# Summing the scan's states in turned form in both loop halves of a decoder kernel, with the work behind it one loop step later

## The reference, cut to what matters

```python
u = silu(x_proj); dt = softplus(u @ W_dt + b_dt); Bm, Cm = split(u @ W_x + b_x)
def step(h, inp):                       # over the 128 tokens
    h = h * exp(dt_t[..., None] * A) + (dt_t * u_t)[..., None] * B_t[:, None, :]
    y_t = einsum('bds,bs->bd', h, C_t) + D_param * u_t
    return (h, y_t)
y = y * silu(z)
return y @ W_out + b_out
```

## Time and profile before

| | |
|---|---|
| median of 3 executions | 391.0 us (390.95 to 392.38) |
| the profiled execution, whole | 391.27 us |
| its span in the trace | 389.3 us |
| TensorE busy with matmuls | 326.6 us (84%) |
| VectorE busy | 309.9 us (80%) |
| GpSimd busy | 217.4 us |
| ScalarE busy | 213.5 us |
| the scan loop | first scan starts at 157.2 us, last at 280.0 us |

### The profile page before, as it was taken

One profiled execution on the slowest core, in us unless ns is written; L12 is line 12 of the kernel. 1 busy time (PEld: TensorE's weight loads), 2 busy tenths in 40 slices (PEclk: granted clock), 3 DMA queues, 4 the chain that ended last, 5 costly groups with the idle time before them and its releaser, 6 DMA issues. The chain is left out here.

```text
span 389.3 us, 5280 instructions
## 1 busy us (share of the span) xinstructions
PE 326.6 (84%) x1666; PEld 227.7 (58%) x1666; DVE 309.9 (80%) x630; ACT 213.5 (55%) x467; POOL 217.4 (56%) x223
## 2 busy tenths in 40 slices
PE   5636929779768889889998998988799989999992
PEld 2432419778546465533343586555598857989872
DVE  0799999998666977999999989999958724763934
ACT  2626131222135959857769627786465657675741
POOL 3499999997124050579899999788602610100111
PEclk9956958999999999989999999999999999999997
DMA  8900000000000001334534443444200000000010
GB/s 272 412 7 1 0 3 0 2 1 2 0 0 2 1 0 45 121 108 138 157 111 162 134 142 118 152 136 134 83 3 0 2 0 0 3 3 0 0 29 27
DMA packets 11521, 24.41 MB, mean 63 GB/s; under 512 B 1231, under 2 KB 2255, under 8 KB 11239
## 3 DMA queue, kind: packets, MB, share of 16 engines
q1 hardware_dynamic: 11495, 24.09, 18.7%
HBM read 23.50 MB, written 0.59 MB: 62 GB/s over the span
## 5 line engine op out<-in xcount | busy, mean ns | idle before, releaser
L1062 POOL TENSOR_TENSOR arena<-arena 128x512 f32<-128x512 f32 x63 | 80.1, 1282 | 28.1 <-DVE arena L688 25.8
L688 DVE TENSOR_TENSOR_SCAN arena<-arena,ps 128x512 f32<-128x512 f32 x64 | 77.2, 1208 | 0.1
L1321 ACT ACTIVATE arena<-arena,neg_a 128x508 f32<-128x508 f32 x64 | 43.2, 712 | 8.4 <-DVE arena L688 6.9
L681 DVE TENSOR_TENSOR ps<-arena,ps 128x512 f32<-128x512 f32 x64 | 43.2, 677 | 1.4 <-PE ps L1763 1.2
L1103 POOL TENSOR_TENSOR rstd<-veps,mhalf 128x4 f32<-128x4 f32 (+2 forms) x6 | 4.8, 810 | 68.8 <-DVE veps L813 35.8
L1597 PE MATMUL ps<-arena,first_in 128*128 128x128 f32 (+1 forms) x256 | 32.0, 287 | 12.5 <-POOL arena L936 12.5
L725 DVE TENSOR_REDUCE arena<-ps 128x2 f32<-128x496 f32 x32 | 21.4, 668 | 25.1 <-PE ps L1830 25.1
L1597 PEld LDWEIGHTS ps<-arena,first_in 128*128 128x128 f32 x256 | 30.9, 202 | 13.8 <-issue 8.1
L1782 PE MATMUL ps<-arena,first_in 128*128 128x512 f32 x64 | 34.2, 616 | 0.5 <-POOL arena L1062 0.5
L1763 PE MATMUL ps<-arena,pick_wide 96*128 96x512 bf16 x64 | 24.5, 388 | 10.3 <-DVE arena L688 9.7
L1371 ACT ACTIVATE first_in<-ps 128x256 f32<-128x256 f32 x32 | 12.4, 387 | 33.2 <-PE ps L1856 33.1
(11 more groups left out here) (296 smaller groups left out, 830.8 us busy)
## 6 DMA issues: line engine op xcount, KB each, us to landing
arena<-c_rows_dram SPq DMA_DIRECT2D x64, 256.0 KB, 3.2
fold_in<-in_fold_dram SPq DMA_DIRECT2D x1, 2056.0 KB, 11.2
late_in<-in_late_dram SPq DMA_DIRECT2D x1, 1423.5 KB, 17.7
early_in<-in_early_dram SPq DMA_DIRECT2D x1, 921.5 KB, 13.1
xres<-in_x_dram SPq DMA_DIRECT2D x1, 512.0 KB, 14.3
kv_ctx<-in_context_dram SPq DMA_DIRECT2D x1, 480.0 KB, 7.1
first_in<-in_first_dram SPq DMA_DIRECT2D x1, 465.0 KB, 3.4
rows_in<-in_rows_dram SPq DMA_DIRECT2D x1, 384.0 KB, 14.8
```

The lines of the kernel that those rows point to most:

```text
L681: tt(chain(q), dtu[:, n, cols(g)], chain(q), ALU.mult).then_inc(S("drive"), 1)
L688: nc.vector.tensor_tensor_scan(hist[:, q % NBUF], fade[:, q % NFADE], chain(q), 0.0, ALU.mult, ALU.add).then_inc(S("scan"), 1)
L1062: tt(seen[:, q % NBUF], hist[:, q % NBUF], c_wide[:, q % NBUF], ALU.mult).then_inc(S("read_out"), 1)
L1321: act(fade[:, q % NFADE].rearrange("p (b t) -> p b t", t=T)[:, :, 1:], dt[:, n, cols(g)].rearrange("p (b t) -> p b t", t=T)[:, :, 1:], ACT ...
```

## The change

In the first loop half the sum over states is now made as in the second. `skip_term` and `accumulate` lose their branches for the first half. `y_out`, `turn_back` and `gate_turned` run for blocks 0 and 1 as well, and `gate_first` and `gate_second` are gone. `turn_back` of block 0 stands in step 30 and of block 1 in step 34, `gate_turned` of block 0 in step 31 and of block 1 in step 35, and block 1 gets a `y_out` in step 34. Block 1 is turned back within bank 5, from which it was copied. Most of what follows in the second half, from the output projection on, stands one step later; `turn_back(2)`, `gate_turned(2)`, the weight folding and two residual additions stay where they were.

```diff
         def y_back(m):
-            return bank(0 if m == 2 else 6)
+            return bank((0, 5, 0, 6)[m])
...
-            def gate_first():
-                ve.wait_ge(S("y0_out"), 1)
-                ve.wait_ge(S("gz"), 1)
-                tt(yg[:, 0, cols(0)], yg[:, 0, cols(0)], gz[:, 0, cols(0)], ALU.mult).then_inc(S("y_gated"), 1)
-            def gate_second():
-                ve.wait_ge(S("seen_used"), NK4)
-                ve.wait_ge(S("gz"), 2)
-                tt(yg[:, 1, cols(0)], y_bank(1), gz[:, 1, cols(0)], ALU.mult).then_inc(S("y_gated"), 1)
             def gate_turned(m):
-                ve.wait_ge(*after("y_back", m - 1))
+                ve.wait_ge(*after("y_back", m + 1))
                 ve.wait_ge(S("gz"), m + 1)
-                tt(yg[:, m % 2, cols(1)], y_back(m), gz[:, m % 2, cols(1)], ALU.mult).then_inc(S("y_gated"), 1)
+                at = cols(m // 2)
+                tt(yg[:, m % 2, at], y_back(m), gz[:, m % 2, at], ALU.mult).then_inc(S("y_gated"), 1)
...
                 if q == 31:
-                    gate_first()
-                if q == NK4 + 2:
-                    gate_second()
-                if q == NK4 + 4:
+                    gate_turned(0)
+                if q == NK4 + 3:
+                    gate_turned(1)
+                if q == NK4 + 5:
                     landed(4, 0, 4)
...
-                if q == NS + 2:
-                    y_out(0)
-                if q == NK4 + NS + 2:
-                    y_out(2)
+                if q % NS == 2 and q > NS:
+                    y_out(q // NS - 1)
...
             def skip_term(n, g):
-                if g == 0:
-                    mm(y_bank(n), diag_d[:, n], u4[:, n, cols(g)], start=True, stop=False)
-                else:
-                    for b in range(HB):
-                        mm(y_bank(n)[:, b * T:(b + 1) * T], u4[:, n, (HB + b) * T:(HB + b + 1) * T], diag_d[:, n],
-                           start=(b == 0), stop=False)
+                for b in range(HB):
+                    mm(y_bank(n)[:, b * T:(b + 1) * T], u4[:, n, (g * HB + b) * T:(g * HB + b + 1) * T], diag_d[:, n],
+                       start=(b == 0), stop=False)
...
-                if p < NK4:
-                    ins = mm(y_bank(p // NS), ident, seen[:, p % NBUF], start=False, stop=last)
-                else:
-                    for b in range(HB):
-                        ins = mm(y_bank(p // NS)[:, b * T:(b + 1) * T], seen[:, p % NBUF, b * T:(b + 1) * T], ident,
-                                 is_transpose=True, start=False, stop=last and b == HB - 1)
+                for b in range(HB):
+                    ins = mm(y_bank(p // NS)[:, b * T:(b + 1) * T], seen[:, p % NBUF, b * T:(b + 1) * T], ident,
+                             is_transpose=True, start=False, stop=last and b == HB - 1)
...
-                if q == NK4 + 3:
+                if q == 30:
+                    turn_back(0)
+                if q == NK4 + 2:
+                    turn_back(1)
+                if q == NK4 + 4:
                     pe.wait_ge(S("kv_ctx"), 2)
                     residual_in(4, 0, 4)
                     output4(0, 4, range(HB), landed=True)
-                if NK4 + 4 <= q < NK4 + 9:
+                if NK4 + 5 <= q < NK4 + 10:
                     stay_awake(2, 6)
```

More of the change, by code:

```diff
@@ L290, in decoder @@
         CTX_BANKS = (4, 6)
-        QUERY_STEPS = [NK4 + k for k in (11, 12, 13, 15, 16, 21, 23, 25)]
+        QUERY_STEPS = [NK4 + k for k in (12, 13, 14, 16, 17, 22, 24, 26)]
         folded = [tiles["fold"][:, k * HW:(k + 1) * HW] for k in range(4)]
@@ L765, in _ @@
                     gate_turned(2)
-                if q == NK4 + 22:
+                if q == NK4 + 23:
                     shift(2)
-                if q == NK4 + 24:
+                if q == NK4 + 25:
                     inverse5(2).then_inc(S("inverse5"), 1)
-                if q == NK4 + 26:
+                if q == NK4 + 27:
                     shift(3)
-                if q == NK4 + 28:
+                if q == NK4 + 29:
                     inverse5(3).then_inc(S("inverse5"), 1)
@@ L1076, in _ @@
                     latent_scale(0)
-                if q == NK4 + 16:
+                if q == NK4 + 17:
                     scaled_latents(0, 0)
-                if q == NK4 + 19:
+                if q == NK4 + 20:
                     scaled_latents(0, 1)
@@ L1461, in _ @@
                     query_out(0, QUERY_STEPS.index(q))
-                if q == NK4 + 15:
+                if q == NK4 + 16:
                     exponentials(0)
-                if q == NK4 + 17:
+                if q == NK4 + 18:
                     scaled5(0)
-                if q == NK4 + 18:
+                if q == NK4 + 19:
                     exponentials(1)
                     turned_out(0)
-                if q == NK4 + 20:
+                if q == NK4 + 21:
                     scaled5(1)
-                if q == NK4 + 23:
+                if q == NK4 + 24:
                     exponentials(2)
                     turned_out(1)
-                if q == NK4 + 25:
+                if q == NK4 + 26:
                     scaled5(2)
-                if q == NK4 + 27:
+                if q == NK4 + 28:
                     mixed_out(0)
                     exponentials(3)
-                if q == NK4 + 28:
+                if q == NK4 + 29:
                     turned_out(2)
-                if q == NK4 + 29:
+                if q == NK4 + 30:
                     scaled5(3)
                     exponentials(4)
-                if q == NK4 + 30:
+                if q == NK4 + 31:
                     mixed_out(1)
@@ L1861, in output5 @@
                 if u == 0:
-                    pe.wait_ge(S("y0_out"), 3)
+                    pe.wait_ge(S("y0_out"), 4)
                     pe.wait_ge(S("fold_vo"), 2)
@@ L1982, in _ @@
                     query(0, QUERY_STEPS.index(q + 1))
-                if q == NK4 + 13:
+                if q == NK4 + 14:
                     similar(0)
-                if q == NK4 + 16:
+                if q == NK4 + 17:
                     similar(1)
-                if q == NK4 + 17:
+                if q == NK4 + 18:
                     turn_probabilities(0)
@@ L1990, in _ @@
                     turn_back(2)
-                if q == NK4 + 21:
+                if q == NK4 + 22:
                     pe.wait_ge(S("y_gated"), NH + 1)
                     similar(2)
-                if q == NK4 + 22:
+                if q == NK4 + 23:
                     turn_probabilities(1)
-                if q == NK4 + 25:
+                if q == NK4 + 26:
                     similar(3)
-                if q == NK4 + 26:
+                if q == NK4 + 27:
                     mix_context(0)
-                if q == NK4 + 27:
+                if q == NK4 + 28:
                     turn_probabilities(2)
                     similar(4)
-                if q == NK4 + 29:
+                if q == NK4 + 30:
                     mix_context(1)
                     turn_probabilities(3)
-                if q == NK4 + 30:
+                if q == NK4 + 31:
                     similar(5)
```

23 lines of the change are left out of this document (12 added, 11 removed).

## The result

The changed kernel takes 390.73 us (median of 22 executions, 389.07 to 392.57). In the same comparison the kernel before took 391.9 (390.86 to 394.77, 22 executions). The ratio is 0.9969, with a 95% interval of 0.9955 to 0.9983: 1.2 us, or 0.3%, faster. That is less than the 0.5% that counted as telling, and less than half of the 2.5 us in the forecast. The predicted time of 388.5 was too low by 2.2 us. Of that, 0.9 us is the starting point, which was 391.0 in three executions and is 391.9 in 22; the other 1.3 us is gain that did not come.

What follows compares the result with a forecast made beforehand. VectorE was taken to bound the loop, TensorE costing only through five waits. The terms 0.75 + 0.3 + 0.37 + 1.25 + 0.15 - 0.3 = 2.5 us, off 391.0, gave 388.5 us, range 387.3 to 391.3.

Steps and rivals of the forecast that it cites:

- (b): VectorE's 0.30 us wait before 174.44, behind a plain accumulation at the lower clock; 0.3 us of gain counted.
- (a): VectorE's waits of 0.25 and 0.34 us before 188.70 and 190.85, for a late widening, both go: 0.75 us gained.
- block 0's gate: Gate on VectorE reading two SBUF operands, 0.82 us; the new form with one from PSUM gains 0.15 us.
- (c): VectorE's 0.29 us wait before 227.27, from TensorE's backlog of steps 31 to 34, goes: 0.37 us gained.
- projection and statistics: VectorE's 1.27 us wait for the output projection shrinks to about 0.1, one step later: 1.25 us gained.
- new wait: VectorE before block 1's gate, waiting for TensorE's turning back: 0 to 0.6 us, 0.3 us taken as loss.
- moved work: Norm, queries, attention rounds and GpSimd's powers one step later, meeting unmoved work only in steps 50 and 63: no cost.
- 2.9 + 0.4 = 3.3: Upper end of the gain in us, if all is gained and no wait is new: about 387.7 us.
- the second rival: Clock falls briefly in two thin stretches, costing in steps 12 to 15 or 28 to 34: 389.1 to 390.5; chance 0.2.
- The first rival: TensorE's backlog goes, but the big wait before the statistics stays: 389.5 us; chance 0.2.
- the third: Clock stays low into TensorE's loaded steps, 12 to 18 and 28 to 36: 395.4 us if through six; chance 0.08.

Runs made afterwards that it cites:

- veps_psum: Changed kernel with the small addition behind the statistics (L396) in another form, one operand from PSUM, epsilon left out for that norm: 389.7 us, ratio 0.9955.
- changed_again: The changed kernel without any edit, timed and profiled a second time: 390.6 us, ratio 0.9965 to the kernel before.
- turns_only: Changed kernel with the turns and new gates, but what follows in the second half back at its old steps: 390.93 us, ratio 0.9979.
- before_third: The kernel before without any edit, a third profile: 392.2 us in one execution.
- shift_only: Kernel before with its old sum and gates, but all that follows in the second half one loop step later: 391.02 us, ratio 0.9987.
- turns_and_veps: Changed kernel with filler transposes in step 4 and steps 24 to 27, and L396 reading PSUM without that norm's epsilon: 389.44 us, ratio 0.9947.
- hold_both_turns: Changed kernel with filler transposes on TensorE, 12 in step 4 and 6 in each of steps 24 to 27: 389.91 us, ratio 0.995.
- best: Changed kernel with filler transposes in step 4, steps 8 to 11 and 24 to 27, and GpSimd adding the epsilon instead of VectorE: 390.0 us, ratio 0.9965.

## Why the prediction was half right

By sections of the loop, means over the three profiles of each kernel, in us gained (the differences of the rows in the table):

| section | terms of the sum | predicted | measured |
|---|---|---|---|
| to scan 9 | (b) | +0.3 | -0.5 |
| scans 9 to 17 | (a) | +0.75 | +0.78 |
| scans 17 to 34 | block 0's gate | +0.15 | +0.23 |
| scans 34 to 38 | (c), projection and statistics, new wait | +1.32 | +0.69 |
| scans 38 to 63 | moved work, "Nothing" | 0 | 0.0 |
| sum | | 2.5 | 1.2 |

The upper end of the forecast, "2.9 + 0.4 = 3.3", has no terms behind it. The largest values that the terms allow, 0.75 + 0.38 + 0.37 + 1.35 + 0.15, make 3.0 us.

**What held.** (a): both waits went. (c) and the 1.25 of the projection: both waits went whole, 0.29 and 1.27 by their brackets in the earlier trace rows, and veps_psum shows 1.65 us for scans 34 to 38 where these terms make 1.62. The new wait before block 1's gate was 0.38, 0 and 0.34 us in three profiles, against 0.3 taken and 0 to 0.6 allowed; it is absent where the low clock before it ended earlier or did not come. The gate of block 0 and the moved work were as said, and the 109.4 us behind the loop didn't move.

**The first step that failed** is in (b): "But the low clock may last longer with less work on TensorE, so I count 0.3 of it." The doubt was right, and the number was a gain all the same. The three profiles put scan 9 at +0.70, -0.26 and +0.62, and those of before at 0, -0.61 and +0.13. The turns did shorten an accumulation as worked out. Where the low clock lasted 3.4 us, as long as before, they gave what the wait in (b) is worth: scan 9 at -0.26, -0.45 and -0.46 (changed_again, turns_only, veps_psum) against 0, +0.13 and -0.13 with the old form (before, before_third, shift_only). Where it lasted 6.8 us, the two loaded steps cost more than that. So the step that failed is the low stretch's length, and how large the loss is on average depends on how often the long one comes. The -0.5 in the table has it in two profiles of three. With veps_psum and turns_only, which don't differ from the changed kernel up to scan 9, it is two of five, and the mean of scan 9 is +0.03 against -0.16 before: a loss of 0.2 in place of 0.5. This is the second rival, with its price (0.5 to 2 us back) but not its place: I looked for it in steps 12 to 15 and behind step 27, and it came before them, from 170.0 to 176.9, where steps 6 and 7 of TensorE are loaded with L1715, two passes of 512 columns in each. The timeline of TensorE in the changed kernel:

```profile
172.37 1.91 PE L1715 MATMUL ps<-xcol,late_in 128*128 128x512 f32 x2
174.07 0.63 PE L1751 MATMUL ps<-arena,pick_wide 96*128 96x512 bf16 x1
174.50 1.06 PE L1767 MATMUL ps<-first_in,arena 128*128 128x128 f32 x4
175.35 1.77 PE L1715 MATMUL ps<-xcol,late_in 128*128 128x512 f32 x2
176.96 0.38 PE L1751 MATMUL ps<-arena,pick_wide 96*128 96x512 bf16 x1
```

From one widening to the next this is 2.96 and 2.89 us where VectorE needs 1.71 for a step. In the second thin stretch the low clock was nearly free, as the rival said that it would be: up to 0.36 us, at the gate.

**The second step that failed** is one that the sum doesn't have. The statistics one step later were priced by the wait ahead of them and by nothing else. Their last instruction, 0.17 us on 4 columns, came to start inside a GpSimd product, and took 0.9, that is 0.72 to 0.73 us more, in every kernel with the turns, the new place and the old form. In shift_only, where it starts later in the product, it took 0.56, and in veps_psum the loss is gone. In the trace of before the product ends 0.03 us ahead of it. The views to look at were there: the timeline of GpSimd beside that of VectorE.

The two together, 0.8 and 0.7 us in the three profiles of the table, are more than the 1.3 us that are missing; the rest of the terms came out 0.2 better. That the terms account for the whole is partly luck, since the first of them moves with the choice of profiles. The first rival did not occur, since no wait was left before the projection. Nor did the third: the clock came back in loaded steps each time.

What stays open is what makes the clock fall in one execution and not in the next of the same kernel. The first scan itself starts anywhere from 156.8 to 158.3 us, and the five profiles above relate the length of the low stretch to its distance from that start, but no run here varied the one to see the other move.

## What to carry to other kernels

Where work is moved by a step, lay the timelines of VectorE and GpSimd over each other at the new place: a tiny instruction that reads SBUF alone can wait there for a whole product, and no view of waits lists it, because it counts as busy. Where TensorE is made thinner, the clock has to be priced together with the loaded steps behind the thin place, and from more than one execution; turns serve as filler as well as matmuls do. And a gain on the slowest engine ends at the next one: here it was GpSimd together with filler matmuls queued behind its product, once VectorE had gained 2.4 to 2.8 us.

## What the runs showed of the hardware that I had not expected

- VectorE's `TENSOR_SCALAR` on 128x4 f32 in SBUF took 0.17 us beside an idle GpSimd, and 0.36, 0.56, 0.89 and 0.90 us when it started inside one of GpSimd's 1.27 us products, ending 0.02 to 0.03 us after the product each time. A `SCALAR_TENSOR_TENSOR` of the same size with one operand in PSUM took 0.16 us inside such a product.
- f32 turns as filler kept the granted clock at 1.00 at the two places where it fell in all five profiles with the turns and no filler. In turns_and_veps it was 1.00 through the whole loop of 120 us; in hold_both_turns and best it fell once, near 258.5, for 3.4 us.
- The same program had its low clock at other places in other executions: in three profiles of the changed kernel the stretch near 172 lasted 3.4 us once and 6.8 us twice, and one of three profiles of the kernel before had none. The loops of the one lay 1.1 us apart, those of the other 0.6 us.
